# Low-times-low products in the channel mixing and in the grouped convolution of a two-layer kernel

## The chip, the cores and the metric

One core of a Trainium2 chip. The metric is the device time of one execution in microseconds (us), as the median of several runs. Engines: TensorE (PE, with its weight loads shown apart as PEld), VectorE (DVE), ScalarE (ACT), GpSimd (POOL), and SyncE (SP), which issues the transfers.

## The reference, cut to what matters

The input `x` has 64 batches of 64 channels with 1024 positions. Two layers are added to it, one after the other; each first works on the channels and then multiplies the 1024 positions with wide matrices.

```python
# layer 0: mixing of the 64 channels by a matrix of its own for each batch
out = jnp.einsum('boi,bih->boh', agg_w, x) + agg_b[:, :, None]
# then: gate (32 columns), lora_A (128), weight (1024), top-2 routing, lora_B
# layer 1: grouped convolution along the positions, 4 groups of 16 channels, 9 taps
out = lax.conv_general_dilated(x, weight, window_strides=(STRIDE,), padding=[(PAD, PAD)],
                               dimension_numbers=('NCH', 'OIH', 'NCH'), feature_group_count=GROUPS)
# then: Wq, Wk (256 columns each), A (128), W (1024), softmax over 8 experts, Bm
```

## The kernel before

All products are made at single precision out of two halves. A number is split into a high half (rounded to the matrix engine's fast 32-bit format, `fp32r`) and a low half (what is left). A full product of two such numbers has four parts: high times high, high times low, low times high and low times low. The helper `split_product` (lines 1347 to 1351) issues the first three as three matrix products into one accumulator, each with its own weight load, and leaves the fourth out.

The 64 batches lie in 32 tiles of 128 rows (two batches of 64 channels).

**First stage (`phase_a`, lines 1473 to 1484).** Because the mixing works on channels and the wide matrices on positions, the kernel multiplies with the wide matrices first (`main`, 8 pieces of the contraction in 3 banks of 384, 416 and 384 columns, so 24 products a bank) and mixes afterwards. `mix` (lines 1435 to 1455) multiplies the 128 x 128 matrix of the tile's two batches (`mix_hl`, high and low) with the split result of a bank (`yh`, `yl`, in the tile `part`). ScalarE makes the high half (L751), VectorE the low one (L991), and after the mixing VectorE adds the bank to `row` (L999). `mix` waits for the low half (`y_lo`), for the matrix (`mix_ready`) and for the bank to be read (`mix_read`); its last product increments `mix_done`. The order on TensorE is written out: main bank 1, mix bank 0 of the tile two ahead, main bank 2, mix bank 1, main bank 0 of the tile three ahead, mix bank 2. There are 32 x 3 = 96 mixings.

**Second stage (`phase_b`, lines 1574 to 1632).** For each tile TensorE makes the products with the second layer's wide matrices (`second`: 4 banks of 320, 320, 512 and 512 columns, 24 products each), and between them two halves of the convolution of the next tile (`conv(t + 1, 0)` and `conv(t + 1, 1)`).

In the convolution the tile's values are the stationary side (split, in `part`, `mix_hl` and `ones`), and the band matrix of the taps is the moving side: `conv_hl[:, m, group, s, :]`, with s = 0 for its high and s = 1 for its low half, 128 columns each. From the third tile on (lines 1517 to 1526) a half has two groups, each with three windows w. For window 1 the high stationary half meets both rows and both halves, 512 columns (L1522), and the low stationary half meets both rows of the high half alone, 256 columns (L1524). For windows 0 and 2 these are 256 and 128 columns. The two accumulators (s = 0 and s = 1) are added by VectorE when it reads them out (L1228, L1235); then ScalarE and VectorE split the sum into `lhs_h` (L884) and `lhs_l` (L1239), which the next tile's `second` products read. Tiles 0 and 1 (lines 1506 to 1516) are done by batch: 4 groups and 2 windows a half, each with a product of 256 columns (L1511) and one of 128 (L1513).

Engines order their work among each other by semaphores alone; every engine's instructions run in the order of the code.

Of the kernel before, what the change touches and what calls it, by code (L numbers as in the profile page):

```python
# [25 lines left out]
P = 128  # L26
# [46 lines left out]
def program(nc, a, out):  # L73
    with ExitStack() as ctx:
        def sb(name, shape, dt=F32):
            return ctx.enter_context(nc.sbuf_tensor(name, shape, dt))

        def psum(name, shape):
            return ctx.enter_context(nc.psum_tensor(name, shape, F32))
# [26 lines left out]
        yh, yl = (part[:, s, :].rearrange("p (k n) -> p k n", k=3) for s in range(2))  # L106
# [15 lines left out]
        conv_hl = sb("conv_hl", [P, 2, GRP, 2, P], F32R)  # L122
# [9 lines left out]
        mix_hl = sb("mix_hl", [P, XB, 2, P], F32R)  # L132
# [43 lines left out]
        def set_halves(part_of, h, w):  # L176

            n = part_of * 6 + h * 3 + w
            return [sets[n][:, 0:P], sets[n][:, P:2 * P]] if n < len(sets) else last_set
# [11 lines left out]
        def by_batch(t):  # L191
            return isinstance(t, int) and t < 2

        def run_of(t, part_of, b, g):

            g0, flat = [r for r in runs01[t][part_of, b] if r[0] <= g][-1]
            return flat[:, (g - g0) * WS:(g - g0 + 1) * WS]

        def stationary(t, part_of, h, g, w):

            if by_batch(t):
                return run_of(t, part_of, h, g)[:, 64 * w:64 * w + P]
            return set_halves(part_of, h, w)[g]
# [11 lines left out]
        ps = psum("ps", [P, 8, 512])  # L215
# [38 lines left out]
        def banks(name):  # L254
            return [sem(f"{name}_{k}") for k in range(3)]

        main_done, y_hi, y_lo = banks("main_done"), banks("y_hi"), banks("y_lo")
        mix_done, mix_read = banks("mix_done"), banks("mix_read")
# [51 lines left out]
        def item(t, k):  # L310

            return (k - 1) * AHEAD + t - (TILES - AHEAD)

        def is_end(t, k):

            return isinstance(t, int) and t >= TILES - AHEAD and k > 0
# [7 lines left out]
        def y_slot(t, k):  # L324

            if isinstance(t, int) and k == 0 and t in (1, 2):
                return t
            return (1, 2)[item(t, k) % 2] if is_end(t, k) else k

        def slot_before(t, k):  # L330

            if isinstance(t, int) and t < 3 and k == 0:
                return None
            if at(t, 0):
                return 0, k
            if is_end(t, k):
                i = item(t, k)
                return (i + 1, TILES - AHEAD - 1) if i < 2 else (1 + (i - 2) // AHEAD, TILES - AHEAD + (i - 2) % AHEAD)
            return k, t - 1

        def mix_bank(t, k):
            if k == 0 and isinstance(t, int) and t in (1, 2):
                return BC[2 - t]
            return BM_END[item(t, k) % 2] if is_end(t, k) else BM0[k]
# [15 lines left out]
        def at(t, n):  # L360

            return isinstance(t, int) and t == n

        def before_end(t, n):

            return not isinstance(t, int) or t + n < TILES
# [979 lines left out]
        def _(pe):  # L1346
            def split_product(out_ap, lhs, rhs, first=True, last=True):

                pe.matmul(out_ap, lhs[0], rhs[0], start=first, stop=False, skip_group_check=True)  # L1349
                pe.matmul(out_ap, lhs[0], rhs[1], start=False, stop=False, skip_group_check=True)  # L1350
                return pe.matmul(out_ap, lhs[1], rhs[0], start=False, stop=last, skip_group_check=True)  # L1351
# [83 lines left out]
            def mix(t, b, k):  # L1435

                if k == 0:
                    pe.wait_ge(mix_ready, t * 2 + 2)
                pe.wait_ge(y_lo[k], t + 1)
                if at(t, 0):  # L1440
                    pe.wait_ge(wsum_ready, k + 1)
                elif k == 0 and at(t, 1):
                    pe.wait_ge(aggc_ready, 2)
                elif k == 0 and at(t, 2):
                    pe.wait_ge(attc_ready, 1)
                elif not is_end(t, k):
                    pe.wait_ge(mix_read[k], t)
                elif item(t, k) == 0:
                    pe.wait_ge(y_lo[0], TILES)
                elif item(t, k) > 1:  # L1450
                    before_k, before_t = slot_before(t, k)
                    pe.wait_ge(mix_read[before_k], before_t + 1)
                slot, n = y_slot(t, k), COLS0[k]
                split_product(ps[:, mix_bank(t, k), 0:n], (mix_hl[:, b, 0, :], mix_hl[:, b, 1, :]),
                              (yh[:, slot, 0:n], yl[:, slot, 0:n])).then_inc(mix_done[k], 1)

            pe.wait_ge(zeroed, 1)
            pe.wait_ge(wide_set, 1)
# [10 lines left out]
            column_sums(1)  # L1469
            pe.wait_ge(zeroed, 4)  # L1470
            mix(0, 0, 0)

            def phase_a(t, b, it):
                main(t, b, 1)
                if at(t, 0):
                    mix(1, 1, 0)
                    column_sums(2)
                mix(t + 2, (b + 2) % XB, 0)
                main(t, b, 2)
                mix(t, b, 1)  # L1480
                main(t + AHEAD, (b + AHEAD) % XB, 0)
                mix(t, b, 2)
# [19 lines left out]
            def conv(t, h):  # L1502
                pe.wait_ge(z_lo, t * 24 + h * 12 + 12)
                if h == 1 and before_end(t, 1):
                    pe.wait_ge(x1_ready, t * 2 + 4)
                if by_batch(t):
                    for g in range(GRP):
                        dst = ps[:, (BP1, BP0)[h][g // 2], (g % 2) * 256:(g % 2) * 256 + 256]
                        for m in range(2):
                            both = conv_hl[:, 1 - m, g, :, :].rearrange("p s n -> p (s n)")  # L1510
                            pe.matmul(dst, stationary(t, 0, h, g, m), both, start=(m == 0), stop=False,  # L1511
                                      skip_group_check=True)
                            mm = pe.matmul(dst[:, 0:P], stationary(t, 1, h, g, m), conv_hl[:, 1 - m, g, 0, :],  # L1513
                                           start=False, stop=(m == 1), skip_group_check=True)
                    mm.then_inc(conv_done, 1)
                    return
                for g in range(2):
                    dst = ps[:, (BP1, BP0)[h][g], :].rearrange("p (k s n) -> p k s n", k=2, s=2)
                    both = conv_hl[:, :, 2 * h + g, :, :]
                    for w, out_k, rows in ((1, slice(0, 2), slice(0, 2)), (0, slice(0, 1), slice(1, 2)),  # L1520
                                           (2, slice(1, 2), slice(0, 1))):
                        pe.matmul(dst[:, out_k], stationary(t, 0, h, g, w), both[:, rows], start=(w == 1), stop=False,  # L1522
                                  skip_group_check=True)
                        mm = pe.matmul(dst[:, out_k, 0, :], stationary(t, 1, h, g, w), both[:, rows, 0, :], start=False,  # L1524
                                       stop=(w == 2), skip_group_check=True)
                mm.then_inc(conv_done, 1)

# [38 lines left out]
            main(T3, B3, 2, 0, 2)  # L1566
            pe.wait_ge(*low_of(N_CONV))
            conv(0, 0)
            mix(T2, B2, 2)
            conv(0, 1)  # L1570
            main(T3, B3, 2, 2, 8)
            pe.wait_ge(*low_of(N_LB1))

            def phase_b(t, u, it):
# [33 lines left out]
                if nxt:  # L1608
                    conv(t + 1, 0)
# [91 lines left out]
```

## Time and profile before

| | |
|---|---|
| median of 3 runs | 1264.6 us (1264.4 to 1265.13) |
| profiled execution | 1264.31 us |
| its span | 1262.5 us |
| products and weight loads on TensorE | 6967 each |
| mean granted TensorE clock | 1.000 |
| TensorE, VectorE, ScalarE, GpSimd busy | 1257.6, 847.4, 306.6, 236.5 us |

The profile is of one execution. Its span goes from the first to the last instruction that it shows; the rest of the execution's time lies around it. TensorE's products are pipelined: their shown ends are modelled and reach into the products behind them, so the durations of neighbouring products overlap. Starts are measured. The view by groups has one line for each source line, operation and shape.

### The profile page before, as it was taken

What the parts mean: (1) busy time and instruction counts of PE and PEld (TensorE: products, weight loads), DVE (VectorE), ACT (ScalarE), POOL (GpSimd) and SP (SyncE); (2) the same over time, 40 slices, a digit from 0 to 9 for tenths busy, and PEclk for the clock granted to TensorE, in tenths of its full rate; (3) what the DMA queues carried; (4) which work ended last, traced back from release to release, by engine and by line L of the source; (5) the groups of instructions that cost most, each with busy time, mean ns of one, the idle gap of its engine ahead of it and who ended that gap; (6) DMA issues with size and microseconds to landing.
All of it is one profiled execution on the core that took longest, in us unless ns stands there. A gap on an engine that the chain in (4) does not pass through costs nothing.

```text
span 1262.5 us, 21215 instructions
## 1 busy us (share of the span) xinstructions
PE 1257.6 (100%) x6967; PEld 1165.7 (92%) x6967; DVE 847.4 (67%) x2171; ACT 306.6 (24%) x654; POOL 236.5 (19%) x170
## 2 busy tenths in 40 slices
PE   9999999999999999999999999999999999999998
PEld 8999999999999999888889889888888888988987
DVE  7887867666667667756765765675676576576563
ACT  6323322222322234211211121121121112112110
POOL 1244522232322322011001001001100100100100
PEclk9999999999999999999999999999999999999999
DMA  8354433433333367434223323322423332332310
GB/s 275 122 169 146 154 110 116 138 118 120 109 110 117 105 221 220 123 90 123 71 85 114 83 71 108 104 71 89 123 71 88 117 77 71 112 100 71 99 42 34
DMA packets 84889, 141.55 MB, mean 112 GB/s; under 512 B 6769, under 2 KB 53361, under 8 KB 84849
## 3 DMA queue, kind: packets, MB, share of 16 engines
q1 hardware_dynamic: 84704, 140.78, 36.7%
q8 instruction: 22, 0.36, 0.1%
q10 hardware_dynamic: 144, 0.26, 0.1%
q14 instruction: 19, 0.15, 0.0%
HBM read 88.57 MB, written 52.45 MB: 112 GB/s over the span
## 4 chain that ended last, share of the span: by engine, by line
PE 100%; DVE 0%; issue 0%
PE ps L1349 30%; PE ps L1351 30%; PE ps L1350 30%; PE ps L1522 5%; PE ps L1524 2%; PE ps L1390 0%; PE ps L1511 0%; PE ps L1357 0%; PE ps L1488 0%; PE ps L1618 0%; PE ps L1402 0%; PE ps L1513 0%; PE ps L1403 0%; PE ps L1408 0%; PE ps L1406 0%; PE ps L1409 0%
## 5 line engine op out<-in xcount | busy, mean ns | idle before, releaser
L1349 PE MATMUL ps<-weights,lhs_h 128*128 128x512 f32 (+3 forms) x1408 | 497.8, 354 | 0.0
L1350 PE MATMUL ps<-weights,lhs_h 128*128 128x512 f32 (+3 forms) x1408 | 488.4, 347 | 0.0
L1351 PE MATMUL ps<-weights,lhs_l 128*128 128x512 f32 (+3 forms) x1408 | 488.4, 347 | 0.0
L1349 PEld LDWEIGHTS ps<-weights,lhs_h 128*128 128x128 f32 x1408 | 264.3, 188 | 23.7 <-issue 0.3
L1351 PEld LDWEIGHTS ps<-weights,lhs_l 128*128 128x128 f32 x1408 | 264.3, 188 | 21.5
L1350 PEld LDWEIGHTS ps<-weights,lhs_h 128*128 128x128 f32 x1408 | 264.9, 188 | 19.8
L714 POOL TENSOR_TENSOR xo<-row,wsum 128x512 f32<-128x512 f32 x60 | 76.8, 1305 | 647.5 <-DMA out_x<-xo 647.5
L1349 PE MATMUL ps<-weights 128*128 128x384 f32 (+1 forms) x376 | 128.6, 342 | 0.0
L1350 PE MATMUL ps<-weights 128*128 128x384 f32 (+1 forms) x376 | 127.9, 340 | 0.0
L1351 PE MATMUL ps<-weights 128*128 128x384 f32 (+1 forms) x376 | 127.8, 340 | 0.0
L1235 DVE TENSOR_TENSOR whole<-ps,whole 64x256 f32<-64x256 f32 x240 | 101.4, 422 | 7.7
L1228 DVE TENSOR_TENSOR whole<-ps,bias_in 64x256 f32<-64x256 f32 x240 | 101.3, 422 | 6.5
L751 ACT ACTIVATE part<-ps 128x384 fp32r<-128x384 f32 (+1 forms) x96 | 47.9, 499 | 231.0 <-PE ps L1351 231.0
L1522 PE MATMUL ps<-conv_hl,part 128*128 128x512 f32 x360 | 99.9, 344 | 0.0
L884 ACT ACTIVATE lhs_h<-whole 128x512 fp32r<-128x512 f32 x64 | 40.5, 633 | 235.6 <-DVE whole L1235 228.4
L991 DVE TENSOR_TENSOR part<-ps,part 128x384 fp32r<-128x384 f32 (+1 forms) x96 | 54.2, 565 | 57.8 <-ACT part L751 56.3
L667 POOL TENSOR_TENSOR row<-row,biased 128x800 f32<-128x800 f32 x31 | 61.3, 1976 | 124.4 <-DMA row<-in_xr 100.4
L1291 DVE TENSOR_TENSOR staging<-ps,mixw 128x256 f32<-128x256 f32 x32 | 13.6, 425 | 96.9 <-PE ps L1351 96.6
L1146 DVE TENSOR_TENSOR row<-ps,row 128x512 f32<-128x512 f32 x60 | 41.5, 692 | 53.0 <-PE ps L1351 52.7
L1319 DVE TENSOR_TENSOR xo<-ps,xo 128x512 f32<-128x512 f32 x64 | 43.2, 692 | 45.1 <-PE ps L1351 45.0
L1522 PEld LDWEIGHTS ps<-conv_hl,part 128*128 128x128 f32 x360 | 67.6, 188 | 6.3
L1349 PEld LDWEIGHTS ps<-weights 128*128 128x128 f32 x376 | 70.5, 188 | 0.6 <-issue 0.3
(201 smaller groups left out, 1629.7 us busy)
## 6 DMA issues: line engine op xcount, KB each, us to landing
row<-spill SPq DMA_DIRECT2D x30, 576.0 KB, 4.4
z<-x_round SPq DMA_DIRECT2D x64, 256.0 KB, 5.1
out_x<-xo SPq DMA_DIRECT2D x31, 512.0 KB, 2.7
xo<-in_xt SPq DMA_DIRECT2D x30, 512.0 KB, 3.4
x_round<-row SPq DMA_DIRECT2D x60, 256.0 KB, 2.0
row<-in_xr SPq DMA_DIRECT2D x31, 400.0 KB, 3.2
spill<-row SPq DMA_DIRECT2D x31, 400.0 KB, 3.7
staging<-in_w SPq DMA_DIRECT2D x9, 832.0 KB, 6.3
```

Source lines behind the costliest of these rows:

```text
L667: pool.tensor_tensor(dst, dst, biased[:, BANK0:OUT0], ALU.add).then_inc(row_ready12, 1)
L714: pool.tensor_tensor(natural[:, PAD * (1 - h):PAD * (1 - h) + J // 2, :], src[:, q].rearrange("p (s i) -> p s i", i=P), b1bc[:, q].rearran ...
L751: act.activation(yh[:, slot, 0:COLS0[k]], ps[:, BY0[slot], 0:COLS0[k]], ACT.Copy).then_inc(y_hi[k], 1)
L991: dve.tensor_tensor(yl[:, slot, 0:n], ps[:, BY0[slot], 0:n], f32(yh[:, slot, 0:n]), ALU.subtract).then_inc(y_lo[k], 1)
L1146: dve.tensor_tensor(base[:, q], ps[:, BP0[h], :], base[:, q], ALU.add).then_inc(x1_ready, 1)
L1228: dve.tensor_tensor(where_to[to, b], parts[q, :, k, 0], add[to, b, :, None, :].to_broadcast([64, 2, J, GC]), ALU.add).then_inc(conv_part, 1)
L1235: dve.tensor_tensor(where_to[to, b], parts[q, :, k, 1], where_to[to, b], ALU.add).then_inc(conv_read, 1)
L1319: dve.tensor_tensor(o, ps[:, BQ[2 + h], :], o, ALU.add).then_inc(y_read, 1)
L1349: pe.matmul(out_ap, lhs[0], rhs[0], start=first, stop=False, skip_group_check=True)
L1350: pe.matmul(out_ap, lhs[0], rhs[1], start=False, stop=False, skip_group_check=True)
L1351: return pe.matmul(out_ap, lhs[1], rhs[0], start=False, stop=last, skip_group_check=True)
L1522: pe.matmul(dst[:, out_k], stationary(t, 0, h, g, w), both[:, rows], start=(w == 1), stop=False, skip_group_check=True)
```

## The change

`mix` gets a fourth product: the low half of the mixing matrix times the low half of the bank's rows. It is the last of the group, and `mix_done` is incremented by it. In the convolution no product is added; those with the low stationary half get the low half of the band matrix as well, so they are as wide as their high neighbours: 256 instead of 128 columns, and for window 1 512 instead of 256. What is added there goes into the accumulator s = 1.

```diff
--- before.py
+++ after.py
@@ -1451,8 +1451,10 @@
                     before_k, before_t = slot_before(t, k)
                     pe.wait_ge(mix_read[before_k], before_t + 1)
                 slot, n = y_slot(t, k), COLS0[k]
-                split_product(ps[:, mix_bank(t, k), 0:n], (mix_hl[:, b, 0, :], mix_hl[:, b, 1, :]),
-                              (yh[:, slot, 0:n], yl[:, slot, 0:n])).then_inc(mix_done[k], 1)
+                dst = ps[:, mix_bank(t, k), 0:n]
+                split_product(dst, (mix_hl[:, b, 0, :], mix_hl[:, b, 1, :]), (yh[:, slot, 0:n], yl[:, slot, 0:n]), last=False)
+                pe.matmul(dst, mix_hl[:, b, 1, :], yl[:, slot, 0:n], start=False, stop=True,
+                          skip_group_check=True).then_inc(mix_done[k], 1)
 
             pe.wait_ge(zeroed, 1)
             pe.wait_ge(wide_set, 1)
@@ -1510,8 +1512,8 @@
                             both = conv_hl[:, 1 - m, g, :, :].rearrange("p s n -> p (s n)")
                             pe.matmul(dst, stationary(t, 0, h, g, m), both, start=(m == 0), stop=False,
                                       skip_group_check=True)
-                            mm = pe.matmul(dst[:, 0:P], stationary(t, 1, h, g, m), conv_hl[:, 1 - m, g, 0, :],
-                                           start=False, stop=(m == 1), skip_group_check=True)
+                            mm = pe.matmul(dst, stationary(t, 1, h, g, m), both, start=False, stop=(m == 1),
+                                           skip_group_check=True)
                     mm.then_inc(conv_done, 1)
                     return
                 for g in range(2):
@@ -1521,7 +1523,7 @@
                                            (2, slice(1, 2), slice(0, 1))):
                         pe.matmul(dst[:, out_k], stationary(t, 0, h, g, w), both[:, rows], start=(w == 1), stop=False,
                                   skip_group_check=True)
-                        mm = pe.matmul(dst[:, out_k, 0, :], stationary(t, 1, h, g, w), both[:, rows, 0, :], start=False,
+                        mm = pe.matmul(dst[:, out_k], stationary(t, 1, h, g, w), both[:, rows], start=False,
                                        stop=(w == 2), skip_group_check=True)
                 mm.then_inc(conv_done, 1)
```

## Rows read from the trace of the kernel before

**Rows 1.** The page's busy times of the engines, and the granted clock in 40 slices

```profile
PE 1257.6 (100%) x6967; PEld 1165.7 (92%) x6967; DVE 847.4 (67%) x2171; ACT 306.6 (24%) x654; POOL 236.5 (19%) x170
...
PEclk9999999999999999999999999999999999999999
```

**Rows 2.** The view of waits, TensorE alone: us in total, times, longest

```profile
PE ps L1357 <- DVE weights L1030: 1.6, 1, 1.6
```

**Rows 3.** The chain that ended last, its last piece: start us, us, what

```profile
1259.26 0.69 DVE xo L1319
```

**Rows 4.** Timeline, TensorE, convolution of one tile: start us, duration us, line, shapes

```profile
813.59 0.39 PE L1522 MATMUL ps<-conv_hl,part 128*128 128x512 f32 x1
813.82 0.28 PE L1524 MATMUL ps<-conv_hl,part 128*128 128x256 f32 x1
...
814.05 0.22 PE L1524 MATMUL ps<-conv_hl,part 128*128 128x128 f32 x1
814.10 0.34 PE L1522 MATMUL ps<-conv_hl,part 128*128 128x256 f32 x1
814.28 0.22 PE L1524 MATMUL ps<-conv_hl,mix_hl 128*128 128x128 f32 x1
814.34 0.45 PE L1522 MATMUL ps<-conv_hl,part 128*128 128x512 f32 x1
814.63 0.28 PE L1524 MATMUL ps<-conv_hl,part 128*128 128x256 f32 x1
...
815.15 0.45 PE L1349 MATMUL ps<-weights,lhs_h 128*128 128x512 f32 x1
815.43 0.40 PE L1350 MATMUL ps<-weights,lhs_h 128*128 128x512 f32 x1
...
817.94 0.39 PE L1522 MATMUL ps<-conv_hl,part 128*128 128x512 f32 x1
818.17 0.28 PE L1524 MATMUL ps<-conv_hl,mix_hl 128*128 128x256 f32 x1
...
818.41 0.22 PE L1524 MATMUL ps<-conv_hl,mix_hl 128*128 128x128 f32 x1
...
819.79 0.39 PE L1350 MATMUL ps<-weights,lhs_h 128*128 128x512 f32 x1
```

**Rows 5.** Groups by line and shape, TensorE: xcount, busy us, mean ns

```profile
L1522 PE MATMUL ps<-conv_hl,part 128*128 128x256 f32 x240 | 61.1, 306 | 0.0
L1522 PE MATMUL ps<-conv_hl,part 128*128 128x512 f32 x120 | 50.4, 420 | 0.0
...
L1351 PE MATMUL ps<-part,mix_hl 128*128 128x384 f32 x64 | 21.6, 337 | 0.0
...
L1351 PE MATMUL ps<-part,mix_hl 128*128 128x416 f32 x32 | 11.3, 354 | 0.0
```

**Rows 6.** Timeline, TensorE, two channel mixings of the first stage

```profile
253.74 0.34 PE L1349 MATMUL ps<-part,mix_hl 128*128 128x384 f32 x1
...
254.27 0.34 PE L1349 MATMUL ps<-weights,lhs_h 128*128 128x384 f32 x1
...
258.43 0.35 PE L1349 MATMUL ps<-part,mix_hl 128*128 128x416 f32 x1
...
259.00 0.34 PE L1349 MATMUL ps<-weights,lhs_h 128*128 128x384 f32 x1
```

**Rows 7.** Timeline, TensorE's weight loads, in the convolution of rows 4

```profile
814.75 0.19 PEld L1524 LDWEIGHTS ps<-conv_hl,part 128*128 128x128 f32 x1
...
815.09 0.19 PEld L1349 LDWEIGHTS ps<-weights,lhs_h 128*128 128x128 f32 x1
```

**Rows 8.** Timeline, VectorE and then TensorE, the end of the same tile

```profile
823.68 1.36 DVE L1239 TENSOR_TENSOR lhs_l<-whole,lhs_h 128x512 fp32r<-128x512 f32 x2
...
829.29 0.31 PE L1349 MATMUL ps<-weights,lhs_h 128*128 128x320 f32 x1
```

**Rows 9.** Timeline, TensorE, the product of 814.34 one tile earlier

```profile
790.12 0.45 PE L1522 MATMUL ps<-conv_hl,part 128*128 128x512 f32 x1
```

## The prediction

> **What bounds the kernel now.** I read the page's busy times first: TensorE is busy for 1257.6 of 1262.5 us, VectorE for 847.4 [rows 1]. The view of waits, TensorE alone, has one entry, 1.6 us at the start [rows 2]. The chain that ended last runs on TensorE until 1259.2 us, and only the last VectorE addition, 0.69 us, stands behind it [rows 3]. So the program is one unbroken row of matrix products, and its time is the sum of the distances from one product's start to the next one's. The other four engines follow it.
>
> These distances can't be taken from the durations: a 512-column product lasts 0.39 us in the rows, but the next one starts 0.23 us after it [rows 4], because the shown ends are modelled and overlap. Every price below is therefore a difference of start times. The granted clock is at nine tenths or more in all 40 slices [rows 1], which is the 2.4 GHz level; no part of what follows can come from it.
>
> **Part 1, the channel mixing.** One product more for each (tile, bank), with the stationary matrix of the third product and the low half of the moving rows. The groups by shape give 64 mixings of 384 columns and 32 of 416 [rows 5]. Three 384-column products of a mixing take 0.53 us from the first start to the next line's first start, 0.177 each; the 24 main products behind them take 4.16 us, 0.173 each [rows 6]. I take 0.175: 64 x 0.175 = 11.2 us. The 416-column ones take 0.57 us for three, 0.19 each [rows 6]: 32 x 0.19 = 6.1 us. Together 17.3 us (17.0 to 17.5 by the ends of these readings). All of it lies on TensorE's row. That the stationary matrix is the same as in the product before saves nothing: lines 1349 and 1350 share theirs too, each has a weight load of its own, and they stand 0.18 us apart like the rest.
>
> **Part 2, the grouped convolution of 30 tiles.** No instruction is added. In each of 120 groups (120 products of 512 columns on line 1522 [rows 5]) one low product goes from 256 to 512 columns, and two (beside the 240 of 256 columns) from 128 to 256. What matters is that a 128-column product is already dearer than it looks. Its own distance is 0.05 or 0.06 us (814.05 to 814.10, 814.28 to 814.34). But the product behind it holds up its own successor. A 256-column one takes 0.18 us there (814.10 to 814.28), and in the second half two without a narrow one before them take 0.24 us together, 0.12 each (818.17 to 818.41). The main product that follows the last narrow one takes 0.28 us against its usual 0.23 [rows 4]. So a narrow product costs 0.06 + 0.055, about 0.115 us, nearly what a 256-column one costs. The weight loads show why: in this stretch four follow each other in 0.34 us, 0.113 each (814.75 to 815.09) [rows 7], so a product of 0.06 us can't cover the load for its successor, and one of 0.117 us can.
>
> By halves (two groups, 12 products): now, 813.59 to 815.43 is 1.84 us less the 0.23 of one main product, 1.61; the other half, 817.94 to 819.79, 1.85 less 0.23, 1.62 [rows 4]. Afterwards, four 512-column products of 0.23 and eight 256-column ones. The price of the latter is 0.115 by the first half (813.82 to 814.05 for two) and 0.12 by the second [rows 4]; I take 0.117: 0.92 + 0.94 = 1.86 us. That is 0.24 us more a half, and 60 halves make 14.4 us. With 0.115 it is 13.5, with 0.12 it is 15.9.
>
> **Part 3, the convolution of tiles 0 and 1** (by batch; 32 pairs of a 256- and a 128-column product by the code). The same pair takes 0.18 + 0.05 us in part 2 (814.05 to 814.28), and two 256-column products 0.23 or 0.24 [rows 4]. That is 0 to 0.01 a pair, 0 to 0.3 us in all; I take 0.2.
>
> **What waits for it.** The order on all engines stays, no wait is added, and no memory or transfer. Seen from TensorE's own place in the tile, a mixing's result is finished 0.18 us later, and each half of the convolution 0.24 us later. Behind the second half stands VectorE's read-out, which may start up to 0.24 us late; but its last piece, the low half of the next tile's rows, starts at 823.68 and takes 1.36 us, and TensorE needs it at 829.29 [rows 8]. That is a cover of 4.2 us, and none of the delay reaches TensorE. If the cover were gone, such a delay still could not multiply: a chain through the other engines passes each added product once at most, so waits can at most hand on the added time, not add to it.
>
> **Sum.** 17.3 + 14.4 + 0.2 = 31.9 us. The profiled execution took 1264.31 us, with a span of 1262.5 (1.8 us lie around it), and the median of the runs is 1264.6, so 0.3 above it. The span becomes 1294.4, the profiled time 1296.2 and the median 1296.5 us, 2.5% more.
>
> **The rivals.**
> *A, as worked out.* 1296.5 us; by the bounds of the terms +30.5 to +33.7.
>
> *B, width alone counts.* If the lateness behind the narrow products is not their weight load but something that the stage has anyway (its strided read, the change of PSUM bank), it stays, and every widening costs its columns: 256 to 512 0.113 us, 128 to 256 0.117 - 0.06 = 0.057 us. Then the conv gives 120 x (0.113 + 2 x 0.057) = 27.2, the batch tiles 32 x 0.057 = 1.8, and with the mixing +46.3 us: 1310.9 us. Against it: the lateness stands behind each narrow product shown and behind no other, and it reaches even the main product after them, which reads something else (0.28 instead of 0.23), and a 512-column one (814.34 to 814.63) [rows 4]. What remains for it is that the stage never ran without narrow products.
> The Trainium skill (TensorE: Matmul & The Clock Gate, Back-to-back issue gap) gives an isolated gap of N/2.4 + 2.5 ns whatever stands around it; as an estimate from it, the three parts would be 16.0 + 25.6 + 1.7 = 43.3 us, 1307.9 us. The trace has 0.23 us where that rule has 0.216, and 0.18 where it has 0.109.
>
> *C, not slower.* Since modelled ends hide a wait of up to some 0.15 us in TensorE's rows, the product after a mixing could really be waiting for a semaphore (the next tile's halves, or the read-out of the slot before). Then the fourth product would fill that wait. It decides if this wait is at least 0.175 us at each of the 96 mixings; and to reach 1264.6 the same would be needed of 0.24 us in all 60 halves of the convolution. Against it: the distance over the border, 254.27 less 253.74 for three products, is that of a run without any border to within 0.01 us [rows 6], so there is nothing to fill. If the mixing alone were free, it would be 1279.2 us.
>
> **How the numbers follow.** A 0.91, B 0.05, C 0.01 for the whole and 0.01 for the mixing alone, 0.02 for what is not named, such as a late hand-over where the first stage goes over into the second. The forecast is A's, 1296.5. The range takes the bounds of the terms on the lowest and highest run shown: 1264.4 + 30.5 = 1294.9 and 1265.1 + 33.7 = 1298.8, opened a little below for the hundredths to which starts are read: 1294.4 to 1298.8. B lies outside, C too. A run of this kernel tells 0.2%, some 2.5 us, from no change; A and B are both far above it, so slower 0.98, and 0.01 each for the others.
>
> **What would show it.** In the mixing, four products in 0.70 us (384 columns) and 0.76 us (416), and 7063 products instead of 6967. In the convolution, all 256-column products 0.11 to 0.12 us apart, none at 0.17, the main product behind them back at 0.23, a half at 1.86 us. The second stage's period, 24.22 us by the distance of the same product in neighbouring tiles, goes to about 24.7 us [rows 4, 9]. TensorE still without a wait after the start, and VectorE's share lower at the same busy time. If the distances of 0.17 behind 256-column products remain, B is right; if the chain shows VectorE or a wait of TensorE in the middle, the argument on cover is wrong.

## The result, and the profile after

The changed kernel takes 1296.64 us (1296.42 to 1296.73), the kernel before, beside it, 1264.62. The ratio is 1.0252, with a 95% interval of 1.0235 to 1.027: slower by 32.0 us, where 31.9 were forecast (1296.5 us). The profiled execution has a span of 1294.8 us against 1262.5.

The page of the kernel after, busy times and granted clock, answers to [rows 1]:

```profile
PE 1289.4 (100%) x7063; PEld 1192.1 (92%) x7063; DVE 848.9 (66%) x2171; ACT 306.8 (24%) x654; POOL 234.8 (18%) x170
...
PEclk9999999999999999999999999999999999999999
```

TensorE has 96 products and 31.8 us of busy time more, VectorE has the same work in a longer span. TensorE's waits [rows 2], in the view of waits of the kernel after (us in total, times, longest):

```profile
PE ps L1357 <- DVE weights L1030: 1.6, 1, 1.6
PE ps L1402 <- ACT weights L736: 0.5, 1, 0.5
```

The second one ends 9 us after the start, where the first weights are still being loaded and split. The changed lines do not run there, and all of the runs below show such an entry, of 0.2 to 1.4 us in all, whatever their edit; so I don't count it as part of the change. No wait stands anywhere behind it, and the end of the chain is the same VectorE addition as in [rows 3]:

```profile
1291.57 0.69 DVE xo L1319
```

From its end to the end of the span 2.5 us pass in both kernels, which the prediction's account of the chain leaves out and which don't change.

The mixing in TensorE's timeline (start us, duration us), to be held against [rows 6]. Line 1456 is the added product:

```profile
262.17 0.34 PE L1349 MATMUL ps<-part,mix_hl 128*128 128x384 f32 x1
262.35 0.34 PE L1350 MATMUL ps<-part,mix_hl 128*128 128x384 f32 x1
262.52 0.34 PE L1351 MATMUL ps<-part,mix_hl 128*128 128x384 f32 x1
262.70 0.34 PE L1456 MATMUL ps<-part,mix_hl 128*128 128x384 f32 x1
262.87 0.34 PE L1349 MATMUL ps<-weights,lhs_h 128*128 128x384 f32 x1
...
267.04 0.35 PE L1349 MATMUL ps<-part,mix_hl 128*128 128x416 f32 x1
...
267.61 0.34 PE L1456 MATMUL ps<-part,mix_hl 128*128 128x416 f32 x1
267.79 0.34 PE L1349 MATMUL ps<-weights,lhs_h 128*128 128x384 f32 x1
```

Four products from 262.17 to 262.87 are 0.70 us, 0.175 each; four of 416 columns take 0.75 us (267.04 to 267.79). The added one takes 0.17 us at 384 columns and 0.18 us at 416. Its stationary matrix is the one of the product before it, and it has a load of its own all the same (7063 of each). But at these widths a product lasts longer than a load (0.113 us [rows 7]), so the price doesn't tell whether a repeated load takes time.

The convolution in the same view, against [rows 4]: the whole first half of one tile, and the borders of the second.

```profile
836.78 0.39 PE L1524 MATMUL ps<-conv_hl,part 128*128 128x512 f32 x1
837.01 0.39 PE L1526 MATMUL ps<-conv_hl,part 128*128 128x512 f32 x1
837.23 0.28 PE L1524 MATMUL ps<-conv_hl,part 128*128 128x256 f32 x1
837.35 0.28 PE L1526 MATMUL ps<-conv_hl,part 128*128 128x256 f32 x1
837.47 0.28 PE L1524 MATMUL ps<-conv_hl,part 128*128 128x256 f32 x1
837.59 0.28 PE L1526 MATMUL ps<-conv_hl,mix_hl 128*128 128x256 f32 x1
837.71 0.39 PE L1524 MATMUL ps<-conv_hl,part 128*128 128x512 f32 x1
...
838.64 0.40 PE L1349 MATMUL ps<-weights,lhs_h 128*128 128x512 f32 x1
838.87 0.39 PE L1350 MATMUL ps<-weights,lhs_h 128*128 128x512 f32 x1
...
841.37 0.39 PE L1524 MATMUL ps<-conv_hl,part 128*128 128x512 f32 x1
...
843.26 0.39 PE L1349 MATMUL ps<-weights,lhs_h 128*128 128x512 f32 x1
```

No distance of 0.17 us is left behind a 256-column product; they stand 0.12 apart. The main product behind the stage is back at 0.23 us (838.64 to 838.87) where it had 0.28. The first half takes 1.86 us (836.78 to 838.64), the second 1.89 us, against 1.61 and 1.62 before by the same reckoning. The stage's period goes from 24.22 us to 24.73:

```profile
812.98 0.39 PE L1524 MATMUL ps<-conv_hl,part 128*128 128x512 f32 x1
```

That is the product of 837.71 one tile earlier; 0.51 us a tile over 30 tiles is 15.3 us. The convolution of tiles 0 and 1, added up from the starts in the two traces, takes 8.17 us after and 7.96 before, 0.2 us more. On VectorE the delay arrives as foretold and goes no further. Its timeline, and TensorE's at the end of the tile, against [rows 8]:

```profile
843.46 1.78 DVE L1228 TENSOR_TENSOR whole<-ps,bias_in 64x256 f32<-64x256 f32 x4 [0.26 <-PE ps L1526]
...
847.09 1.36 DVE L1239 TENSOR_TENSOR lhs_l<-whole,lhs_h 128x512 fp32r<-128x512 f32 x2
...
852.99 0.31 PE L1349 MATMUL ps<-weights,lhs_h 128*128 128x320 f32 x1
```

VectorE now waits 0.26 us for the second half, 30 times and 7.2 us in all; before, this wait wasn't there. TensorE needs the result at 852.99 and has it at 848.45, a cover of 4.5 us.

### The profile page after: what moved, and what is told of

The parts are those of the page before. It is cut to its first block, busy times and chain, and to the rows that moved or that the text cites. A ratio compares the mean times of both kernels' runs of the same rounds, so it can differ in the third digit from the quotient of the medians.

```text
span 1294.8 us, 21407 instructions
## 1 busy us (share of the span) xinstructions
PE 1289.4 (100%) x7063; PEld 1192.1 (92%) x7063; DVE 848.9 (66%) x2171; ACT 306.8 (24%) x654; POOL 234.8 (18%) x170
## 4 chain that ended last, share of the span: by engine, by line
PE 99%; DMA 0%; SPq 0%; DVE 0%; ACT 0%; issue 0%
PE ps L1349 29%; PE ps L1351 29%; PE ps L1350 29%; PE ps L1524 4%; PE ps L1526 4%; PE ps L1456 1%; PE ps L1390 0%; DMA staging<-in_w 0%; PE ps L1513 0%; PE ps L1515 0%; PE ps L1490 0%; PE ps L1620 0%; PE ps L1402 0%; SPq L434 0%; PE ps L1408 0%; PE ps L1403 0%
## 5 line engine op out<-in xcount | busy, mean ns | idle before, releaser
L1524 PE MATMUL ps<-conv_hl,part 128*128 128x512 f32 x360 | 107.0, 319 | 0.0
L999 DVE TENSOR_TENSOR row<-ps,row 128x384 f32<-128x384 f32 (+1 forms) x94 | 52.7, 562 | 28.5 <-PE ps L1456 27.2
```

The costliest lines, as they stand in the source:

```text
L999: dve.tensor_tensor(dst, ps[:, mix_bank(t, k), 0:dst.shape[1]], dst, ALU.add).then_inc(mix_read[k], 1)
```

## The experiments

All start from the kernel before. The times of before in these comparisons were 1265.1 to 1265.6 us, so differences are taken within each comparison. One of them is uncertain by about 1 to 2 us, as the intervals say.

**1. The two parts of the change apart.** First the mixing alone (the first piece of the diff), then the convolution alone (the other two).

> The fourth product in the 96 channel mixings alone, the convolution as before. A (sum of start distances): 64 x 0.175 + 32 x 0.19 = 17.3 us more than before, about 1281.9 us. C (the product fills a wait that the modelled ends hide): no more than before, 1264.6 us. Conv alone and mixing alone should add up to the 32.0 us of the whole change.

> All widenings in the convolution, the mixing with three products. A (a 128-column product already costs its successor's weight load): 14.4 + 0.2 us more than before, about 1279.2 us. B (width alone counts): 27.2 + 1.8 = 29.0 us more, 1293.6 us.

Measured: mixing alone 1281.15 against 1265.55 us, ratio 1.0126 (1.0111 to 1.0142), 15.6 us more. Convolution alone 1280.51 us, ratio 1.0117 (1.0102 to 1.0133), 15.0 us more. Their sum is 30.6 us, the whole 32.0, the same within the intervals. B's 29.0 us for the convolution is far outside; so is C's zero for the mixing.

**2. The convolution's widenings apart.** Narrow alone (`P` to `2 * P` in windows 0 and 2, and by batch), and the middle window alone. Of the first kernel's edit, the part from the third tile on:

```diff
-                        mm = pe.matmul(dst[:, out_k, 0, :], stationary(t, 1, h, g, w), both[:, rows, 0, :], start=False,
-                                       stop=(w == 2), skip_group_check=True)
+                        s = slice(0, 2) if w != 1 else slice(0, 1)
+                        mm = pe.matmul(dst[:, out_k, s], stationary(t, 1, h, g, w), both[:, rows, s], start=False,
+                                       stop=(w == 2), skip_group_check=True)
```

The second has `w == 1` in the place of `w != 1`, and tiles 0 and 1 as before.

> Only the 128-column products are widened to 256 (240 in the loop's tiles, 32 in tiles 0 and 1); those of 256 columns stay, the mixing too. A: 272 x 0.003 us, 1 us more at most, 1264.6 to 1265.6 us, though 34816 columns are added. B: 272 x 0.057 = 15.5 us more, 1280.1 us.

> Only the 120 low products of the middle window are widened, from 256 to 512 columns; the 128-column ones stay. A and B alike: 120 x 0.113 = 13.6 us more, 1278.2 us, for 30720 added columns, fewer than the narrow ones would add. Together with the narrow ones widened it should give the conv alone.

Measured: 272 products twice as wide give 1266.38 against 1265.55 us, ratio 1.0004 (0.9995 to 1.0013), 0.8 us. 120 products twice as wide give 1280.30 us, ratio 1.0115 (1.0100 to 1.0131), 14.8 us. So 34816 added columns cost nothing that could be told from zero (1.6 us at the upper end of the interval), and 30720 added columns cost nearly all of the convolution's price. The timeline of the first kernel shows the exchange:

```profile
816.09 0.28 PE L1525 MATMUL ps<-conv_hl,part 128*128 128x256 f32 x1
816.20 0.28 PE L1522 MATMUL ps<-conv_hl,part 128*128 128x256 f32 x1
816.32 0.28 PE L1525 MATMUL ps<-conv_hl,mix_hl 128*128 128x256 f32 x1
```

The pair of a narrow product and the one behind it, 0.05 + 0.18 us in [rows 4], is 0.11 + 0.12.

**3. The other direction: fewer columns, or none.** If the weight load sets the price, narrowing must not help, and leaving out must save the load's time.

```diff
+                        n = P if w == 1 else 64
+                        mm = pe.matmul(dst[:, out_k, 0, 0:n], stationary(t, 1, h, g, w), both[:, rows, 0, 0:n], start=False,
+                                       stop=(w == 2), skip_group_check=True)
```

> From the kernel before, the 240 low products of 128 columns in the convolution are cut to 64 columns; the other 64 columns of the low-times-high product of the outer windows are left out, the weight loads stay. A (the weight load sets the price): no gain, within 1 us of 1264.6 us. B (width counts): 240 x 0.027 = 6.4 us less, 1258.2 us.

> From the kernel before, the 240 low products of 128 columns get 192 (the low-times-low part reaches half of the channels of a group pair, the other half stays left out). A (a product costs the larger of its successor's weight load, 0.114 us, and its own columns, 0.09 us at 192): no change, 1264.6 to 1265.5 us at this chip's base of 1264.6. B (width counts): 240 x 0.027 = 6.4 us more, 1271.0 us.

For the third, `continue` stands ahead of the low product for windows 0 and 2, and the last high product closes the group.

> From the kernel before, the same 240 products are left out with their weight loads (the low-times-high product of the outer windows is missing). A: each costs 0.06 + 0.055 us, so 240 x 0.114 = 27.4 us less, 1237.2 us. B (the lateness belongs to the stage and stays, only 0.06 us each go): 14.4 us less, 1250.2 us.

Measured, with the 128 columns of the kernel before as the middle value:

| low product of the outer windows | us | before beside it | ratio, interval |
|---|---|---|---|
| left out | 1239.01 | 1265.41 | 0.9791 (0.9778 to 0.9805) |
| 64 columns | 1267.79 | 1265.41 | 1.0020 (1.0011 to 1.0029) |
| 192 columns | 1266.09 | 1265.13 | 1.0009 (1.0000 to 1.0018) |
| 256 columns (with tiles 0 and 1) | 1266.38 | 1265.55 | 1.0004 (0.9995 to 1.0013) |

From 128 to 256 columns the time is flat within 1 us, and 64 columns gain nothing; that kernel is even 2.4 us slower, where no change beyond 1 us was expected (see the last section). Leaving the 240 products out saves 26.4 us, 0.110 each. A had 27.4, B 14.4. The timeline of the kernel with 64 columns:

```profile
814.80 0.19 PE L1525 MATMUL ps<-conv_hl,part 128*128 128x64 f32 x1
814.83 0.36 PE L1522 MATMUL ps<-conv_hl,part 128*128 128x256 f32 x1
815.03 0.19 PE L1525 MATMUL ps<-conv_hl,mix_hl 128*128 128x64 f32 x1
```

And of the one with 192:

```profile
815.10 0.25 PE L1529 MATMUL ps<-conv_hl,part 128*128 128x192 f32 x1
815.19 0.31 PE L1522 MATMUL ps<-conv_hl,part 128*128 128x256 f32 x1
815.33 0.25 PE L1529 MATMUL ps<-conv_hl,mix_hl 128*128 128x192 f32 x1
```

The narrow product's own distance is 0.03, 0.05 and 0.09 us at 64, 128 and 192 columns; its successor's is 0.20, 0.18 and 0.14. The pair always takes 0.23 us. What the one saves the other waits. The wait doesn't show as idle time: it lies inside the shown duration of the product behind the narrow one, which for 256 columns is 0.28 us without a narrow product before it, and 0.31, 0.34 and 0.36 us behind one of 192, 128 and 64 columns [rows 4].

**4. Can a wide product hide the load?** The six products of a group in another order, so that a narrow one stands right behind the widest and the loads would have room, if they could run further ahead:

```diff
+                    for n, (high, w) in enumerate(((1, 1), (0, 0), (0, 1), (0, 2), (1, 0), (1, 2))):
```

> From the kernel before, the same six products of each group in another order: high 512, low 128, low 256, low 128, high 256, high 256, so that a narrow product's successor could have been loaded while a wide one ran. A (a load starts only when the product before its own starts, one deep): a narrow product costs 0.114 us wherever it stands, no change within 1 us of 1264.6. If loads could run ahead by two, the 0.055 us behind each of 240 narrow products would go: 13 us less, 1251.4 us.

Measured: 1265.87 against 1265.13 us, ratio 1.0006 (0.9997 to 1.0015). This order doesn't buy the load off either; others were not tried. Its timeline, the first half (a row with x2 is two merged neighbours, a 128- and a 256-column product):

```profile
814.44 0.39 PE L1524 MATMUL ps<-conv_hl,part 128*128 128x512 f32 x1
814.67 0.39 PE L1527 MATMUL ps<-conv_hl,part 128*128 128x128 f32 x2
814.90 0.22 PE L1527 MATMUL ps<-conv_hl,mix_hl 128*128 128x128 f32 x1
...
816.06 0.39 PE L1349 MATMUL ps<-weights,lhs_h 128*128 128x512 f32 x1
816.29 0.39 PE L1350 MATMUL ps<-weights,lhs_h 128*128 128x512 f32 x1
```

A narrow product and the 256-column one behind it take 0.23 us here too (814.67 to 814.90), although a 512-column product runs just before them. To the second main product the half takes 1.85 us (814.44 to 816.29), against 1.84 in [rows 4].

**5. Is there slack at the mixing?** The added product issued twice, so five in each mixing (the low-times-low part is counted twice).

> From the kernel before, the mixing gets its fourth product twice (five products), the convolution as before. A: another 17.3 us on top of the mixing alone, so 34.6 us more than before, 1299.2 us: TensorE has no slack anywhere near the mixings. C: the first of the two is hidden and the second is not, at most 17.3 us more, 1281.9 us.

Measured: 1298.59 against 1265.41 us, ratio 1.0266 (1.0252 to 1.0280), 33.2 us more. The second added product costs as much as the first (15.6, then 17.6 more, 16.6 on average). Nothing was hidden, and C is out for the mixing.

## Why the prediction was right

**What bounds.** TensorE's unbroken row, read off the busy times, the waits and the chain, held: the added distances, summed over the traces, come out in the span to within half a microsecond.

**Part 1, the mixing.** Forecast 17.3 us. The added products stand 0.17 to 0.18 us apart from their successors (64 x 0.175 + 32 x 0.18 = 17.0 us by the rows); alone they measured 15.6, doubled 33.2, so 16.6 each. Over all 96 mixings the starts in the trace after sum to 16.9 us more than before. The term was slightly too large: the fourth 416-column product takes 0.18 us, not the 0.19 of the first three.

**Part 2, the convolution.** Forecast 14.4 us. The step that mattered, that a 128-column product costs its successor's weight load and so almost as much as one of 256 columns, is what the runs with 64, 192 and 256 columns show. The size was a little small: 0.51 us a tile instead of 0.48, 15.3 us. The second half takes 1.89 us instead of 1.86; its 512- and 256-column products were both priced a few nanoseconds too low. This error and that of part 1 have opposite signs, and the closeness of 0.1 us in the total is their cancelling, so in part luck; a single comparison of this kind is not that exact anyway (1 to 2 us).

**Part 3.** Forecast 0.2 us, too little for a difference of two times. Tiles 0 and 1 were widened together with the narrow ones of the others, at 0.8 us for all; the sums over the traces give 0.2 us for them.

**What waits for it.** VectorE waits 0.26 us a tile for the later second half, and TensorE does not wait for VectorE. (One wait of 0.4 us for VectorE stands in the kernel with the convolution alone, and none in the kernel with the whole change.) A case with the cover gone was not tried; that such delays can't multiply stays an argument.

**The rivals.** B fell by experiments 1 to 3: width counts only above what the load takes. The trace of the kernel before already spoke against it, at 64 places outside the convolution that the prediction passed over. There a transposition, also a product of 128 columns, stands among the wide products; one of them (TensorE's timeline):

```profile
510.86 0.27 PE L1618 MATMUL ps<-consts,mixw 128*128 128x128 f32 x1
510.88 0.48 PE L1349 MATMUL ps<-weights,lhs_h 128*128 128x512 f32 x1
511.20 0.40 PE L1350 MATMUL ps<-weights,lhs_h 128*128 128x512 f32 x1
```

Its own distance is 0.02 or 0.03 us, and the 512-column product behind it takes 0.32 instead of 0.23. By such distances each of the 64 adds 0.107 to 0.112 us to the row. So the lateness belongs to narrow products and not to the convolution.

A rival that the prediction does not name is a fixed price for issuing any product, instead of the time of its weight load. No kernel with a narrower stationary side was run. But two pairs of loads with 64 stationary columns stand near the start of the kernel before; one of them, and a pair with 128 columns (timeline of the weight loads, each row two merged neighbours):

```profile
17.72 0.19 PEld L1376 LDWEIGHTS ps<-z 128*64 128x64 f32 x2
17.98 0.29 PEld L1377 LDWEIGHTS ps<-whole,z 64*128 64x128 f32 x2
```

A single load is shown 0.13 us long at 64 columns and 0.18 at 128, and a pair 0.19 and 0.29, so the second of a pair starts about 0.055 us after the first at 64 columns, and 0.11 us after it at 128. Among all the other loads of that trace no two start closer than 0.108 us. This speaks for the load, whose time goes with its columns; four loads are a hint and no experiment.

The gap rule of the Trainium skill (TensorE: Matmul & The Clock Gate, Back-to-back issue gap), which the prediction held beside B, falls for narrow products too. The section says so itself: it calls that gap the isolated one and says that it under-counts at small N because it leaves the weight load out. The prediction applied it to a stream of products, for which it isn't meant. The same page's section LDWEIGHTS (loading the stationary operand) gives columns / 1.2 ns, 107 ns for 128 columns; the pairs here show 0.110 us for a product left out and 0.113 between weight loads [rows 7], so that rule and the trace agree within some 6%.

C fell by experiments 1 and 5 for the mixing, and by experiments 1 and 2 for the convolution.

## What to carry to other kernels

On a TensorE that never waits, price an added product by the distance between starts, not by its shown duration, and look at the product behind it too: a narrow product's cost shows up there. Where each product had its own full weight load, fp32r products of 64, 128 and 192 columns cost about what one of 256 did (some 0.11 us here). Widening them to that was free within 1 or 2 us of the whole time, and narrowing them saved nothing; only leaving the product out did. Each of these narrow products had wider ones around it; several narrow ones in a row were not tried.

## What was not expected

Cutting the narrow products to 64 columns made the kernel slower by 2.4 us (1.0020, interval 1.0011 to 1.0029), though the pairs take the same 0.23 us. The timeline of that kernel behind the convolution:

```profile
816.20 0.39 PE L1350 MATMUL ps<-weights,lhs_h 128*128 128x512 f32 x1
...
818.28 0.39 PE L1350 MATMUL ps<-weights,lhs_h 128*128 128x512 f32 x1
```

Nine main products take 2.08 us there. In the kernel before, the same nine take 2.06:

```profile
815.43 0.40 PE L1350 MATMUL ps<-weights,lhs_h 128*128 128x512 f32 x1
...
817.49 0.39 PE L1350 MATMUL ps<-weights,lhs_h 128*128 128x512 f32 x1
```

So 512-column products of one and the same form run some nanoseconds further apart in one kernel than in the other. Over 60 stretches this difference makes 1.2 us. Summed over all 512-column main products of the second stage that don't stand right behind a convolution, it is 1.7 us, nearly all of the 1.9 by which the two profiled executions differ. What sets it is open; it is of the size by which the terms above were off.
